# Prologue of a two-layer graph attention kernel: x of the first graph is transferred first, and nine of eleven weight pieces are split behind the body's first call

## What is computed

```python
# layer 0
q = (src @ Wq + bq).reshape(Bb, Nn, h, dh).transpose(0, 2, 1, 3)
k = (src @ Wk + bk).reshape(Bb, Nn, h, dh).transpose(0, 2, 1, 3)
attn = softmax(einsum('bhid,bhjd->bhij', q, k) / sqrt(dh))
for r in range(Wv.shape[0]):
    v_r = (src @ Wv[r] + bv[r]).reshape(Bb, Nn, h, dh).transpose(0, 2, 1, 3)
    mask = (adj_matrix == r)[:, None]
    out = out + jnp.einsum('bhij,bhjd->bhid', attn * mask, v_r)
x = _ln(src + out @ Wo + bo, g1, beta1)
x = _ln(x + gelu(x @ W1 + b1) @ W2 + b2, g2, beta2)
# layer 1
e = jnp.einsum('whqd,whkd->whqk', q, k)          # q, k, v = heads(x @ Wq), ...
attn = softmax(where(adj[:, None] > 0, where(e >= 0, e, ALPHA * e), NEG))
out = _layernorm(heads_merged(attn @ v), g1, b1)
out = _layernorm(concatenate([out, x], -1) @ Wffn.T, g2, b2) + x
```

## Time and profile before

| | |
|---|---|
| median of 3 runs | 3253.69 us |
| lowest and highest | 3249.42, 3253.93 us |
| profiled execution, its own time | 3253.88 us |
| its span | 3252.1 us |
| TensorE busy (matmul) | 3119.1 us, 96% |
| VectorE busy | 2710.2 us, 83% |
| ScalarE busy | 2063.7 us, 63% |
| POOL busy | 1473.1 us, 45% |
| first matmul | 40.04 us after the span's start |

### The profile page before, as it was taken

One profiled execution on the slowest core, in us unless ns is written; L12 is line 12 of the kernel. 1 busy time (PEld: TensorE's weight loads), 2 busy tenths in 40 slices (PEclk: granted clock), 3 DMA queues, 4 the chain that ended last, 5 costly groups with the idle time before them and its releaser, 6 DMA issues.

```text
span 3252.1 us, 77634 instructions
## 1 busy us (share of the span) xinstructions
PE 3119.1 (96%) x28930; PEld 2711.1 (83%) x28930; DVE 2710.2 (83%) x4892; ACT 2063.7 (63%) x4300; POOL 1473.1 (45%) x1549
## 2 busy tenths in 40 slices
PE   3999999999999999999999999999999999999996
PEld 2788888888888888888888888888888888888885
DVE  3688888888888888888888888888888888888884
ACT  2566766766766666666666666666666666666664
POOL 1345345345355355355455454454454454454441
PEclk8999999999999999999999999999999999999997
DMA  4333433433433433433433433433433433433431
GB/s 107 82 80 93 104 78 92 105 78 91 107 78 90 107 78 89 108 78 88 109 78 87 109 79 87 108 79 87 105 82 87 104 84 87 103 85 87 101 84 30
DMA packets 217643, 292.63 MB, mean 90 GB/s; under 512 B 31492, under 2 KB 119048, under 8 KB 217608
## 3 DMA queue, kind: packets, MB, share of 16 engines
q1 hardware_dynamic: 217608, 292.16, 38.0%
HBM read 72.89 MB, written 16.78 MB: 28 GB/s over the span
## 4 chain that ended last, share of the span: by engine, by line
PE 81%; DVE 14%; issue 2%; SPq 1%; DMA 1%; ACT 1%; POOL 0%; DVEq 0%; ACTq 0%; POOLq 0%
PE pair L922 44%; PE pair L952 11%; PE pair L976 7%; DVE n L686 5%; PE pair L1035 4%; PE pair L967 4%; PE pair L968 4%; PE pair L940 3%; PE pair L1044 2%; PE pair L927 2%; DVE n L680 2%; DVE n L744 1%; DVE x2t_lo L659 1%; DVE stats L671 1%; SPq L309 1%
## 5 line engine op out<-in xcount | busy, mean ns | idle before, releaser
L396 POOL TENSOR_TENSOR act_r_lo<-act,act_r_hi 128x512 fp32r<-128x512 f32 x256 | 334.8, 1315 | 748.7 <-DVE act_r_hi L886 550.3
L502 ACT ACTIVATE leaky_s<-leaky_s,low_r 128x256 f32<-128x256 f32 x1024 | 505.9, 498 | 2.9 <-DVE low_r L728 2.1
L523 ACT ACTIVATE probs<-pair 128x1024 f32<-128x1024 f32 x256 | 256.7, 1029 | 202.0 <-PE pair L1044 202.0
L402 POOL TENSOR_TENSOR probs<-probs,rel 128x512 f32<-128x512 f32 x256 | 327.2, 1300 | 124.7 <-ACT probs L523 124.7
L732 DVE TENSOR_REDUCE mx_a<-pair 128x4 f32<-128x1024 f32 x256 | 308.0, 1224 | 80.2 <-PE pair L1035 79.9
L496 ACT ACTIVATE leaky_s<-pair 128x1024 f32<-128x1024 f32 x256 | 261.9, 1023 | 159.3 <-PE pair L968 159.3
L724 DVE TENSOR_TENSOR leaky_s<-pair,leaky_s 128x1024 f32<-128x1024 f32 x256 | 312.1, 1219 | 28.5 <-ACT leaky_s L496 28.3
L728 DVE TENSOR_REDUCE low_r<-leaky_s 128x4 f32<-128x1024 f32 x256 | 310.5, 1213 | 2.2
L492 ACT ACTIVATE probs<-pair 128x1024 f32<-128x1024 f32 x256 | 261.8, 1023 | 63.7 <-PE pair L976 59.5
L402 POOL TENSOR_TENSOR leaky_s<-probs,rel 128x512 f32<-128x512 f32 x256 | 301.9, 1208 | 0.1
L390 POOL TENSOR_TENSOR rstd<-mv,eps 128x2 f32<-128x2 f32 x256 | 68.7, 268 | 482.5 <-DVE mv L675 481.6
(11 more groups left out here) (180 smaller groups left out, 9055.7 us busy)
## 6 DMA issues: line engine op xcount, KB each, us to landing
stack_a<-qk SPq DMA_DIRECT2D x768, 128.0 KB, 2.4
stack_r<-qk SPq DMA_DIRECT2D x768, 128.0 KB, 2.4
xt<-in_xT SPq DMA_DIRECT2D x64, 256.0 KB, 3.9
adj_a<-in_adjT SPq DMA_DIRECT2D x64, 256.0 KB, 3.0
xn<-in_x SPq DMA_DIRECT2D x64, 256.0 KB, 3.8
adj_q<-in_adj SPq DMA_DIRECT2D x64, 256.0 KB, 2.8
out<-n SPq DMA_DIRECT2D x64, 256.0 KB, 2.9
probs<-in_w SPq DMA_DIRECT2D x4, 512.0 KB, 5.2
```

The costliest lines, as they stand in the source:

```text
L396: return nc.gpsimd.tensor_tensor(dst, src, hi, ALU.subtract)
L402: last = nc.gpsimd.tensor_tensor(masked_p[g][:, h], probs[:, g, h], rel1[:], ALU.mult)
L502: last = nc.scalar.activation(leaky_s[:, p % SLOTS, k, t], leaky_s[:, p % SLOTS, k, t], ACT.Exp, bias=low_r[:, p, k, t:t + 1], accum_out=d ...
```

## The change

xt of graph 0 becomes SyncE's first transfer (and is left out of the body for graph 0). Behind it come wq, wk, the value weights, two value biases, bq and bk, which is all that `c_loaded` now counts (6 in place of 17). Then the next four weight pieces are issued, and behind them the other eleven constants, counted by a new semaphore `late_loaded`. ScalarE and VectorE cast and split two pieces ahead of the first call of the body and the other nine in `between`, after the first call; ScalarE waits there for all eleven splits, VectorE for the late constants, and makes the rest of `bias_r` there. SyncE issues pieces 7 to 11 in `between`, behind the stack_a transfers and adj_a of graph 0. TensorE's program is unchanged.

```diff
--- before.py
+++ after.py
@@ -252,7 +252,7 @@
         STAGES = 4
         w_hi_done, w_split = sem("w_hi_done"), sem("w_split")
         w_loaded = [sem(f"w_loaded{s}") for s in range(STAGES)]
-        c_loaded = sem("c_loaded")
+        c_loaded, late_loaded, bias_done = sem("c_loaded"), sem("late_loaded"), sem("bias_done")
 
 
         CHUNK = 2 * KT * D
@@ -275,29 +275,12 @@
         v_src = [w["wv"][r].rearrange("(t p) c -> p t c", p=P) for r in range(4)]
         bias_f = probs1[:].rearrange("p h t n -> p (h t n)")[0:1, 2 * KT * D:2 * KT * D + 4 * D]
         v_w = probs1[:].rearrange("p h t n -> p (h t n)")[:, 0:2 * KT * D].rearrange("p (r t c) -> p r t c", r=2, t=KT)
-        N_CONST = 2 + 8 + 3 + 4
+        N_CONST, N_LATE = 2 + 2 + 2, 8 + 1 + 2
         block = ctx.enter_context(nc.Block())
 
 
         @block.sync
         def _(sp):
-
-            for i, (src, hi, lo) in enumerate(pieces[0:FIRST_W]):
-                sp.dma_start(staged(i, src), src).then_inc(w_loaded[i % STAGES], 16)
-
-            sp.dma_start(v_w[:, 0], v_src[0]).then_inc(c_loaded, 16)
-            sp.dma_start(v_w[:, 1], v_src[1]).then_inc(c_loaded, 16)
-            for r, row in enumerate(("g1", "e1", "g2", "e2", "lg1", "lb1", "lg2", "lb2")):
-                sp.dma_start(norm[:, r, :], w[row].partition_broadcast(P)).then_inc(c_loaded, 16)
-            sp.dma_start(bq_c, w["bq"]).then_inc(c_loaded, 16)
-            sp.dma_start(bk_c, w["bk"]).then_inc(c_loaded, 16)
-            sp.dma_start(b1_c, w["b1"]).then_inc(c_loaded, 16)
-            for k, row in enumerate((w["bv"][0], w["bv"][1], w["bo"], w["b2"])):
-                sp.dma_start(bias_f[0:1, k * D:(k + 1) * D], row.rearrange("(a c) -> a c", a=1)).then_inc(c_loaded, 16)
-            for i, (src, hi, lo) in enumerate(pieces[FIRST_W:], FIRST_W):
-                if i >= STAGES:
-                    sp.wait_ge(w_split, i - STAGES + 1)
-                sp.dma_start(staged(i, src), src).then_inc(w_loaded[i % STAGES], 16)
 
             parts = qk[:].rearrange("p t i g n -> p (t i) (g n)")
 
@@ -311,6 +294,8 @@
 
             def load(dst, src, graph, form, done):
 
+                if src is xT and isinstance(graph, int) and graph == 0:
+                    return
                 sp.dma_start(dst[:], src[graph - path.general * G].rearrange(form, p=P)).then_inc(done.sem, 16)
 
             def load_x_terms(graph):
@@ -354,7 +339,30 @@
                     sp.wait_ge(ln_done[LN_O].sem, ln_done[LN_O].at(g0))
                     sp.dma_start(out[g0 - path.general * G].rearrange("(t p) c -> p t c", p=P), result[:]).then_inc(stored.sem, 16)
 
-            turns(sp, body)
+            def weights(first, last):
+
+                for i in range(first, last):
+                    if i >= STAGES:
+                        sp.wait_ge(w_split, i - STAGES + 1)
+                    src = pieces[i][0]
+                    sp.dma_start(staged(i, src), src).then_inc(w_loaded[i % STAGES], 16)
+
+            sp.dma_start(xt[:], xT[0].rearrange("(t p) n -> p t n", p=P)).then_inc(ld_xt.sem, 16)
+            weights(0, FIRST_W)
+            sp.dma_start(v_w[:, 0], v_src[0]).then_inc(c_loaded, 16)
+            sp.dma_start(v_w[:, 1], v_src[1]).then_inc(c_loaded, 16)
+            for k in range(2):
+                sp.dma_start(bias_f[0:1, k * D:(k + 1) * D], w["bv"][k].rearrange("(a c) -> a c", a=1)).then_inc(c_loaded, 16)
+            sp.dma_start(bq_c, w["bq"]).then_inc(c_loaded, 16)
+            sp.dma_start(bk_c, w["bk"]).then_inc(c_loaded, 16)
+            weights(FIRST_W, STAGES + FIRST_W)
+            for k, row in enumerate((w["bo"], w["b2"]), 2):
+                sp.dma_start(bias_f[0:1, k * D:(k + 1) * D], row.rearrange("(a c) -> a c", a=1)).then_inc(late_loaded, 16)
+            sp.dma_start(b1_c, w["b1"]).then_inc(late_loaded, 16)
+            for r, row in enumerate(("g1", "e1", "g2", "e2", "lg1", "lb1", "lg2", "lb2")):
+                sp.dma_start(norm[:, r, :], w[row].partition_broadcast(P)).then_inc(late_loaded, 16)
+
+            turns(sp, body, lambda: weights(STAGES + FIRST_W, n_pieces))
             sp.wait_ge(stored.sem, stored.at(G - 1))
             sp.wait_ge(flag_ready, 1)
             found = sp.value_load(flag[0:1, 0:1], min_val=0, max_val=P)
@@ -483,9 +491,19 @@
 
         @block.scalar
         def _(act_e):
-            for i, (src, hi, lo) in enumerate(pieces):
-                act_e.wait_ge(w_loaded[i % STAGES], 16 * (i // STAGES + 1))
-                nc.scalar.activation(hi, staged(i, src), ACT.Copy).then_inc(w_hi_done, 1)
+            def weights(first, last):
+
+                for i in range(first, last):
+                    src, hi, lo = pieces[i]
+                    act_e.wait_ge(w_loaded[i % STAGES], 16 * (i // STAGES + 1))
+                    nc.scalar.activation(hi, staged(i, src), ACT.Copy).then_inc(w_hi_done, 1)
+
+            def other_weights():
+
+                weights(FIRST_W, n_pieces)
+                act_e.wait_ge(w_split, n_pieces)
+
+            weights(0, FIRST_W)
 
             def copy(dst, src):
 
@@ -608,7 +626,7 @@
                     act_e.wait_ge(q_mm.sem, q_mm.at(g3))
                     biased(1, B_K, bk_c).then_inc(qk_hi_done.sem, 1)
 
-            turns(act_e, body)
+            turns(act_e, body, other_weights)
             act_e.wait_ge(flag_ready, 1)
             found = act_e.value_load(flag[0:1, 0:1], min_val=0, max_val=P)
             with act_e.If(found > 0):
@@ -635,21 +653,34 @@
                 nc.vector.tensor_copy(selr[32 * r:32 * r + 32, :], ident[0:32, c0:c0 + H]).then_inc(ready, 1)
             nc.vector.tensor_copy(stack_a[STK:TALL, 1].rearrange("p h n -> p (h n)"),
                                   ones[STK:TALL, 0:1].broadcast_to([TALL - STK, H * N])).then_inc(ready, 1)
+            def weights(first, last):
+
+                for i in range(first, last):
+                    src, hi, lo = pieces[i]
+                    dve.wait_ge(w_hi_done, i + 1)
+                    nc.vector.tensor_tensor(lo, staged(i, src), hi, ALU.subtract).then_inc(w_split, 1)
+
+            def other_weights():
+
+                dve.wait_ge(late_loaded, 16 * N_LATE)
+                nc.vector.tensor_copy(bias_r[0:1, 2 * D:], bias_f[:, 2 * D:]).then_inc(bias_done, 1)
+                dve.wait_ge(bias_done, 1)
+                nc.vector.tensor_tensor(bias_r[32:33, 2 * D:], bias_f[:, 2 * D:], bias_r[0:1, 2 * D:], ALU.subtract).then_inc(bias_done, 1)
+                weights(FIRST_W, n_pieces)
+
             dve.wait_ge(c_loaded, 16 * N_CONST)
             nc.vector.tensor_tensor(bias_f[:, D:2 * D], bias_f[:, D:2 * D], bias_f[:, 0:D], ALU.subtract).then_inc(ready, 1)
             nc.vector.tensor_tensor(v_w[:, 1], v_w[:, 1], v_w[:, 0], ALU.subtract).then_inc(ready, 1)
             dve.wait_ge(ready, 9)
-            nc.vector.tensor_copy(bias_r[0:1, :], bias_f).then_inc(ready, 1)
+            nc.vector.tensor_copy(bias_r[0:1, 0:2 * D], bias_f[:, 0:2 * D]).then_inc(ready, 1)
             for r in range(2):
                 nc.vector.tensor_copy(W["wv"][0][:, :, r * D:(r + 1) * D], v_w[:, r]).then_inc(ready, 1)
             dve.wait_ge(ready, 12)
-            nc.vector.tensor_tensor(bias_r[32:33, :], bias_f, bias_r[0:1, :], ALU.subtract).then_inc(ready, 1)
+            nc.vector.tensor_tensor(bias_r[32:33, 0:2 * D], bias_f[:, 0:2 * D], bias_r[0:1, 0:2 * D], ALU.subtract).then_inc(ready, 1)
             for r in range(2):
                 nc.vector.tensor_tensor(W["wv"][1][:, :, r * D:(r + 1) * D], v_w[:, r],
                                         W["wv"][0][:, :, r * D:(r + 1) * D], ALU.subtract).then_inc(ready, 1)
-            for i, (src, hi, lo) in enumerate(pieces):
-                dve.wait_ge(w_hi_done, i + 1)
-                nc.vector.tensor_tensor(lo, staged(i, src), hi, ALU.subtract).then_inc(w_split, 1)
+            weights(0, FIRST_W)
 
             def flat(ap):
                 return ap[:].rearrange("p a n -> p (a n)")
@@ -891,7 +922,7 @@
                     dve.wait_ge(act_done.sem, act_done.at(g2, 2))
                     nc.vector.tensor_copy(act_hi[:, 1], act[:, 1]).then_inc(act_hi_done.sem, 1)
 
-            turns(dve, body)
+            turns(dve, body, other_weights)
 
             dve.wait_ge(lowest_done.sem, lowest_done.at(G - 1))
             nc.vector.tensor_scalar(bad[:], lowest[:], float(NT * N), None, ALU.is_lt).then_inc(bad_done, 1)
```

## The result

The changed kernel takes **3243.04 us** (median of 20 runs, 3237.29 to 3251.53) against 3252.22 for the one before (20 runs, 3248.37 to 3257.65): a ratio of 0.9974, 95% interval 0.9967 to 0.998, that is 6.5 to 10.7 us less. The forecast was 7.7 to 7.9 less, 3246.0 in a range of 3242.5 to 3251.0. The profiled execution took 3243.39 us.

The account below looks back on a forecast made before the run. TensorE, busy 96%, bounds the steady state, so only the prologue's chain of transfers and splits could gain: 5.3 us to the score sets plus 2.6 in their pace, 3253.88 - 7.9 = 3246.0 us, range 3242.5 to 3251.0.

Parts of the forecast that it names:

- T: Front: moment VectorE gets past c_loaded, 16.93 us before, taken as 9.5 between bounds of 7.5 and 12.4.
- the upper bound: Front: T of 12.4 us if small transfers end with wo and w1's first half, plus a 2.19 us stall.
- Why most of that is lost: TensorE's start to score sets: copy, maxima and late pieces wait, sets start at T + 37.3; 5.3 of 23.4 us gained.
- The pace: Score sets to transposes of the maxima: VectorE, not stack transfers, sets it; 5.9 us for 8.52, 2.6 gained.
- Cover: Behind graph 0's projection: splits of pieces 3 to 6 and late constants, feared at about 27 us, stay off the path.
- From there on ... undiminished: From the transposes of the maxima (60.63 us before) to the end: a shift there arrives at the end undiminished.
- The sum: Whole kernel: 5.3 + 2.6 = 7.9 us off the profiled 3253.88, giving 3246.0.
- the eaten gain: Rival, prologue: late T, a SyncE stall or slow w2 leaves 3.5 to 6.4 us gained, 3247.5 to 3250.4; 37%.
- the clock came back: Rival, prologue: denser score sets raise TensorE's granted clock sooner; 2.8 us more gained, 3243.2; 5%.
- no backlog: Rival, prologue: 4.45 MB of queued transfers at 99 GB/s delay w2's landing from 37.8 to 59 us; 3267; 5%.
- the 0.2% bound: Whole kernel: about 0.2%, 6.5 us, is what a measurement can tell from no change.
- the call of 58%: Whole kernel: 58% chance of being faster by more than 0.2%, from forecast 50, clock 5, whole front 3.

Follow-up runs that it names:

- e1: Changed kernel with only ScalarE's second value copy of graph 0 moved ahead of its nine casts; median 3243.01 us, ratio 0.9967 to the kernel before.
- e3: Changed kernel with SyncE issuing pieces 7 to 10 between graph 0's second and third group of stacks; median 3242.65 us, ratio 0.9963 to the kernel before.
- e2: Changed kernel, but all eleven pieces split ahead of the body; early x and shorter list of constants kept; median 3244.23 us, ratio 0.9965 to the kernel before.
- e4: Changed kernel, but all 17 constants issued ahead; early x and move of nine pieces kept; median 3252.25 us, ratio 0.9995 to the kernel before.
- e5_best: Changed kernel with pieces 3 to 6 split in idle time, 7 to 10 issued before the stacks, value copy early, b1 and norm later; 3234.87 us, repeated 3231.85.
- e8_wf_last: As e5_best, but wf issued behind all twelve stacks and split behind the shift; median 3229.78 us, ratio 0.9929 to the kernel before.

## Why the prediction was right

- **The wait that bounds the front** (c_loaded): the right wait, its size 1 to 1.8 us too high. T was 8.53 and 7.73 in the change's two profiles, and 8.15 to 8.28 in e1 to e3, against 9.5; four of the five lie below the 8.5 at which the forecast's own band began. The 0.9 us between forecast and result at the transposes is this term. bk landed 4.12 us after its issue, while wo and w1 were still moving, so the small transfers did not end with those behind them, as the upper bound had it. The lower end, 7.5, was the nearer one.
- **"Why most of that is lost"**: right: from T to the score sets 37.41 and 37.24 us against 37.3. That close it is by some luck in the terms: w2's half took 4.13 and not 4.5, while T to TensorE's start, its projection and each cast and split were 0.1 to 0.2 longer than their terms, wf 3.83 for 3.77. e1 shows the hold by the copy and the maxima, e3 that by SyncE's order, e2 and e4 that the move as a whole pays less than half a us.
- **The pace**: right: 5.90 us from the first set to the transposes against 5.9, 2.6 gained.
- **Cover**: the late constants arrived earlier than the 27 us that were feared (VectorE went on at 24.68, after 0.68 us of waiting), with the same result, nothing on the path.
- **"From there on ... undiminished"**: not quite. 0.9 us went with the granted clock, and between graph 0's FFN and the end the lead moved by +2.7 and -0.1 us in the two profiles; from the transposes on it moved by +1.8 and -1.1, within the 2 us that the prediction had set as a sign of being wrong. The sum took this as nothing, with a scatter of half a us in the range.
- **The sum.** 7.9 us were forecast and 7.90 stand at the first profile's GELU: that agreement is luck, since T, 1.0 too high, and the 0.9 lost with the clock cancel. And of the 3.0 us between 3246.0 and the measured 3243.04, 1.7 come from the base: the sum starts from one profiled execution of 3253.88 us, and the median of twenty is 3252.22. The gain between the medians is 9.2 us; the forecast's 7.9 lies inside its interval of 6.5 to 10.7.
- **Rivals**: the eaten gain did not come; the clock came back later and not sooner; no backlog (347 GB/s moved at 16 to 18 us, and w2's half landed at 36.6, ahead of the forecast's 37.8). The measured interval, 6.5 to 10.7 us less, has the 0.2% bound at its edge, so the call of 58% was about as sharp as this measurement is.

## What to carry to other kernels

Work that is taken off the front pays only up to the next engine that needs it: follow the first idle engine's *next* wait (here a copy in the following call, the maxima behind it, and a queue whose order put twelve transfers ahead of the weights) before counting the earlier start. Where a change has two halves, cost each alone: here eleven constants taken out of the first wait and issued later were nearly the whole gain, and the larger rearrangement only paid once the pieces went into idle gaps that the same trace shows. A big transfer placed between small ones that set a pace holds these up: in e5_best wf between the stacks put the transposes 2.5 to 2.7 us later than in e8_wf_last, counted from the first landing, where it stood behind them and cost nothing.

## What the runs showed of the hardware that was not expected

**VectorE beside POOL.** In e5_best one subtraction of 1x512 elements, 0.68 us elsewhere, took 1.63 while POOL made xt_lo:

```profile
15.20 1.63 DVE L684 TENSOR_TENSOR bias_r<-probs,bias_r 1x512 fp32r<-1x512 f32 x1
```

```profile
14.93 1.36 POOL L414 TENSOR_TENSOR xt_r_lo<-xt,xt_r_hi 128x512 fp32r<-128x512 f32 x1 [12.23 <-DVE xt_r_hi L822]
```

It ended 0.54 us after POOL's, as if most of it had run only then. The Trainium skill, "SBUF — State Buffer", section "SBUF: two separate sides", has a rule for it: an operation of VectorE with two inputs in SBUF and one of GpSimd that reads SBUF lock each other out for the whole instruction. The trace agrees, here and in the rows at 246 and 249 us above, which overlap POOL's masks: the second, 2.67 us for two operations, is as long as two of the masks, which take 5.32 for four.

**The granted clock.** Kernels that differ in the prologue alone need times up to 1.2 us apart from the transposes to the first GELU (32.41 before, 33.30 and 33.32 in the changed kernel's two, 32.66 in e1, 32.94 in e2, 32.77 in e3, 32.13 in e4). In e5 to e8, taken to TensorE's start on w1, it is 30.78 to 33.12, against 30.70 before; and single falls later took 3 to 4.7 us. A gain of 2 us in the prologue (e1, e3) is plain in the trace's marks and can't be told in the total.

Before its first fall this record can't be taken as it stands. In the kernel after it reads 1.00 up to 26.5 us, yet the pairs of TensorE's first projection start every 0.43 us from 16.3 to 18.4 us and every 0.235 from 20.6 to 22.0: the first is the pace that the same work has where the record reads 0.50 (the product with wo from 74.4 us on).
